# Post-LN transformer layer on one NeuronCore: attention sums of the first layer kept beside each value, and divided after a transfer

## The reference

```python
    x = _layernorm(x + _L0_attn_ref(x, L0_attn_Wqkv, L0_attn_Wo, L0_attn_bo), axis=-1)
    x = _layernorm(x + _L0_ffn_ref(x, ...), axis=-1)

    # _L0_attn_ref
        qkv = x @ Wqkv
        q = apply_rope(q)
        k = apply_rope(k)
        q = q / jnp.sqrt(jnp.sum(q * q, axis=-1, keepdims=True) + 1e-06)
        k = k / jnp.sqrt(jnp.sum(k * k, axis=-1, keepdims=True) + 1e-06)
        attn = jnp.einsum('bthd,bshd->bhts', q, k) / math.sqrt(HD)
        attn = jax.nn.softmax(attn, axis=-1)
        out = jnp.einsum('bhts,bshd->bthd', attn, v).reshape(b, t, d)
        return out @ Wo + bo
```

## Time and profile before

| | |
|---|---|
| median of 3 runs | 1354.19 us (1352.57 to 1356.01) |
| profiled execution, own time | 1358.76 us |
| its span, first to last instruction | 1357.0 us |
| TensorE busy | 1261.1 us, 93% |
| ScalarE busy | 922.6 us, 68% |
| VectorE busy | 793.4 us, 58% |
| GpSimd busy | 238.9 us, 18% |
| mean granted TensorE clock | 0.975 |

### The profile page before, as it was taken

The page is one execution under the profiler, slowest core; times in us unless marked ns, Lnnn a source line. Parts: engine busy times, 40 slices in busy tenths (PEclk is TensorE's granted clock), DMA queues, the critical chain, the costliest instruction groups (busy, mean ns, idle before and its releaser), DMA issues. The chain is left out here.

```text
span 1357.0 us, 20871 instructions
## 1 busy us (share of the span) xinstructions
PE 1261.1 (93%) x7142; PEld 673.0 (50%) x7142; DVE 793.4 (58%) x1876; ACT 922.6 (68%) x1634; POOL 238.9 (18%) x182
## 2 busy tenths in 40 slices
PE   5599999999999898999999999999987899999996
PEld 2133343343343333344434343444333799999996
DVE  5234455455451677787878787877863554444442
ACT  1388788787787465676667666766654477777775
POOL 3212212212211010011111111111101122122121
PEclk8799999999999899999999999999988999999998
DMA  4255342341333121223222222212368321112110
GB/s 156 75 140 109 103 140 65 107 140 59 113 127 95 52 87 63 74 69 87 71 86 72 78 80 68 90 51 92 123 205 231 111 66 57 53 52 59 55 51 5
DMA packets 101087, 122.60 MB, mean 90 GB/s; under 512 B 7347, under 2 KB 86835, under 8 KB 100980
## 3 DMA queue, kind: packets, MB, share of 16 engines
q1 hardware_dynamic: 79302, 89.12, 21.4%
q10 hardware_dynamic: 17248, 19.27, 4.8%
q0 software_dynamic: 4432, 12.87, 3.2%
HBM read 46.89 MB, written 24.27 MB: 52 GB/s over the span
## 5 line engine op out<-in xcount | busy, mean ns | idle before, releaser
L740 ACT ACTIVATE w_space<-bank 128x512 f32<-128x512 f32 x1024 | 560.4, 607 | 281.4 <-PE bank L497 273.3
L956 DVE TENSOR_REDUCE negm<-bank 128x1 f32<-128x512 f32 x512 | 334.1, 684 | 105.4 <-PE bank L529 102.9
L497 PE MATMUL bank<-w_space 96*128 96x512 bf16 (+1 forms) x1024 | 356.6, 387 | 31.2 <-DMA w_space<-work_space 16.0
L514 PE MATMUL bank<-w_space 128*32 128x512 f32 x2048 | 275.4, 610 | 0.2 <-ACT w_space L749 0.2
L497 PEld LDWEIGHTS bank<-w_space 96*128 96x128 bf16 (+1 forms) x1024 | 93.9, 99 | 309.7 <-ACT w_space L740 213.6
L529 PE MATMUL bank<-w_space 96*128 96x512 bf16 x512 | 198.3, 387 | 16.7 <-DVE negm L956 7.0
L692 PE MATMUL bank<-w_space,work_space 128*128 x624 | 141.0, 379 | 0.0
L560 PE MATMUL bank<-work_space,wqkv_sb 128*128 128x512 f32 x256 | 126.5, 620 | 9.4 <-DMA wqkv_sb<-in_w_qkv_dram 6.1
L692 PEld LDWEIGHTS bank<-w_space,work_space 128*128 128x128 f32 x624 | 115.6, 190 | 14.1
L1390 POOL TENSOR_TENSOR work_space<-w_space,work_space 128x1024 bf16<-128x1024 f32 x32 | 68.2, 2132 | 303.5 <-ACT work_space L791 185.2
L529 PEld LDWEIGHTS bank<-w_space 96*128 96x128 bf16 x512 | 50.4, 98 | 91.3 <-DVE negm L956 52.5
(11 more groups left out here) (162 smaller groups left out, 1350.7 us busy)
## 6 DMA issues: line engine op xcount, KB each, us to landing
w_space<-work_space SPq DMA_DIRECT2D x372, 128.0 KB
w_space<-in_w_dram SPq DMA_DIRECT2D x14, 1024.0 KB, 16.0
work_space<-rows_dram SPq DMA_DIRECT2D x39, 256.5 KB, 2.6
work_space<-in_x_t_dram ACTq DMA_DIRECT2D x8, 512.0 KB, 3.8
work_space<-in_x_dram ACTq DMA_DIRECT2D x8, 512.0 KB, 3.8
x_dram<-xo SPq DMA_DIRECT2D x16, 256.0 KB, 4.1
h_dram<-row_sb SPq DMA_DIRECT2D x16, 256.0 KB, 2.2
work_space<-h_dram ACTq DMA_DIRECT2D x8, 512.0 KB, 3.9
```

The lines of the kernel that those rows point to most:

```text
L497: nc.tensor.matmul(bank[:, :], k_stack[0:rows, b % 2, HEADS_AT_ONCE * g + j, kt * P:(kt + 1) * P], q_stack[0:rows, b % 2, HEADS_AT_ONCE * ...
L514: last = nc.tensor.matmul(pv_bank[VW * j:VW * (j + 1), :], v_aug[:, 1 - b % 2, at:at + VW], probs[:, q % PROBS, j, :], start=(kt == 0), st ...
L740: nc.scalar.activation(probs[:, q % PROBS, j, :], st_bank(b, c)[0][:, :], ACT.Exp, scale=SCALE).then_inc(exps, 1)
L956: ve.tensor_reduce(negm[:, c % TT, c // TT:c // TT + 1], mx_ring.bank(b, (g, c))[:, :], axis=AX.X, op=ALU.max, negate=True).then_inc(mx_ri ...
```

## The change

In the first layer the ones now stand beside each value: v_aug holds value, one, value, one, 32 columns per head, so that the attention matmul writes each output row and directly below it a row with the head's sum. ScalarE copies the bank as before, now into o_space. New tasks MV0 to MV3 on SyncE send, per group, the odd partitions (sums) to o_sums, a free part of row_sb, and the even ones (values) to o_rows, a view of on, where four groups make up 2 x 128 rows of channels by 512 tokens. New tasks ON0, ON1 on VectorE, each for two groups, take the reciprocal of 128x512 sums and multiply. That is already the transposed form which WO needs, so TO, TP and their evictions go in the first layer. MV0 of a batch waits for WO1 of the batch before, since the rows share memory. The second layer keeps its transposes and reads values and sums at a step of two.

The tables move WO0 from (9, 3) to (5, 2) and WO1 from (10, 2) to (6, 1). The nine padding transfers move from stage 2 to stage 1, since row_sb is used for sums from there on.

```diff
 ATTENDED = (
-    dict(TO0=(7, 3), TO1=(11, 3), TO2=(15, 3)),
+    dict(MV0=(6, 2), MV1=(9, 2), MV2=(13, 2), ON0=(15, 0)),
 FINISHED = (
-    dict(TO3=(2, 3), TP0=(4, 0), TP1=(6, 3), WO0=(9, 3), WO1=(10, 2), R1=(11, 1), N10=(12, 0),
+    dict(MV3=(1, 2), RS=(2, 3), ON1=(4, 0), WO0=(5, 2), WO1=(6, 1), R1=(11, 1), N10=(12, 0),
          N11=(12, 2), R2=(13, 1), N20=(14, 0), N21=(14, 2)),
...
+        o_sums = (row_sb[:, 1:3, D:2 * D], row_sb[:, 0:TT:3, D:2 * D])
...
+        o_rows = on[:, :, :].rearrange("p t d -> p (t d)").rearrange("p (u t) -> p u t", u=KD)
+        oT = o_space[:, :, :].rearrange("p s d -> p (s d)")
@@ TensorE: pv, WO @@
-                    at = (kt * H + HEADS_AT_ONCE * g + j) * VS
+                    at = (kt * H + HEADS_AT_ONCE * g + j) * VW
...
-                    pe.wait_ge(*ring.empty(b, f"TP{u}"))
+                    if second(b):
+                        pe.wait_ge(*ring.empty(b, f"TP{u}"))
+                    else:
+                        pe.wait_ge(on_ready, 2 * b + 2)
...
+                            rows = turned_of(u)[:, t, k, :] if second(b) else o_rows[:, k, at:at + P]
@@ ScalarE: group_out @@
-                if g:
+                if second(b) and g:
                     act.wait_ge(*o_ring.full(b, f"TO{g - 1}"))
-                elif b:
+                elif b > BATCH:
                     act.wait_ge(*o_ring.full(b - 1, f"TO{GROUPS - 1}"))
+                else:
+                    wait(act, o_moved, 32 * (GROUPS * b + g))
@@ VectorE @@
+                elif kind == "ON":
+
+                    dve.wait_ge(o_moved, 32 * (GROUPS * b + 2 * u + 2))
+                    stepping(ve.reciprocal(o_sums[u], o_sums[u]))
+                    all_steps()
+                    rows = o_rows[:, u, :].rearrange("p (a t) -> p a t", a=2)
+                    ve.tensor_tensor(rows, rows, o_sums[u], ALU.mult).then_inc(on_ready, 1)
@@ SyncE @@
+                elif kind == "MV":
+
+                    sp.wait_ge(oT_ready, GROUPS * b + u + 1)
+                    if b == 0 and u == 2:
+                        sp.wait_ge(padded, 16 * (E + 1))
+                    if b and u == 0:
+                        sp.wait_ge(*o_ring.full(b - 1, "WO1"))
+                    own = slice(u % 2 * (P // 2), (u % 2 + 1) * (P // 2))
+                    sp.dma_start(o_sums[u // 2][own], oT[1:P:2, :].rearrange("p (a t) -> p a t", a=2)
+                                 ).then_inc(o_moved, 16)
+                    sp.dma_start(o_rows[own, u // 2, :], oT[0:P:2, :]).then_inc(o_moved, 16)
...
-                if n == 2:
+                if n == 1:
                     sp.wait_ge(pad_set, 2)
```

49 lines of the change are left out of this document (25 added, 24 removed).

## The result

The changed kernel takes 1385.45 us (median), the kernel before 1354.5 in the runs beside it: a ratio of 1.021, 95% interval 1.019 to 1.024. It is slower by 31 us. One of the changed kernel's four executions took 4286.7 us, for a reason that its numbers do not show, and stays out of the ratio; the other three took 1381.3 to 1385.7. The prediction was 1356.8, range 1344 to 1367: wrong, with the time far above the range.

The account below looks back on a forecast made before the run. TensorE, busy 93% of the span, was taken as the bound. Start +8.5, stage 1 -1.3, stages 2 to 7 -6.6 and crossing +2 gave +2.6 on 1354.2: 1356.8 us, range 1344 to 1367.

Parts of the forecast that it names:

- Removed: On TensorE in each first-layer batch, six groups of four transposes go, 0.44 us each, 2.64 us in all.
- The waits are covered: Between nq and nk, the moved WO0 and WO1 let ScalarE catch up, removing TensorE's 1.31 us of waits per stage.
- The reciprocal: On VectorE, twice per batch, a reciprocal of 128x512 was put at 3.1 us from a row of 16 elements.
- both rivals on it: VectorE's reciprocal: 0.77 us giving about 1344 (chance 0.12), or 4.4 us giving 1365.4 (chance 0.20).
- on_ready and WO0: On TensorE, WO0 waits 1.6 us a stage for VectorE's on_ready at t = 20.1, all scores behind it.
- The stack copies: SyncE's copies start at t = 30.9 instead of 26.7; with MV1 between, the last k copy is issued at 47.3.
- The landing: The last k copy was taken to land 3 us after its issue, at t = 50.3, from other SyncE transfers' 2.2 to 4.1.
- The stage is 50.3 (49.0 to 51.4): Stages 2 to 7 end on the k stack at 50.3 us, 1.1 less each, -6.6 in all.
- The padding: At the start, padding stores moved to stage 1 hold batch 0's k copies: first score at 56, +8.5 (0 to +13).
- the rival of an undisturbed start: At the start, k copies hold their place beside the padding stores; first score near 47.4, total 1348; chance 0.18.
- Stage 1: Stage 1 has no WO and loses three TO groups of transposes: -1.3 us.
- The crossing: Stages 8 and 9, into the second layer: ON pairs +4.9, transpose groups -3.5, VectorE idle time hides a little: +2 (-3 to +5).

Follow-up runs that it names:

- experiment 1: Changed kernel with the nine padding stores made to wait for the first score of stage 1; 1381.2 us, 1.020 of the kernel before.
- experiment 5: Changed kernel with padding stores behind stage 1's first score, ON1 between kA's and kB's products, and WO1's addition behind lq except in the last first-layer batch; 1361.8 us.
- experiment 7: Changed kernel with only the last first-layer batch's division on ScalarE, as exp(-ln s), instead of VectorE's reciprocal; 1385.9 us, 1.025 of the kernel before.
- experiment 8: Kernel before with only the nine padding stores moved from stage 2 to the start of stage 1; 1364.2 us, 1.008 of the kernel before.
- experiment 3: Changed kernel with the first layer's reciprocals left out, rows multiplied by the sums; 1368.0 us, 1.008 of the kernel before.
- kernel 2: Changed kernel with WO0 and WO1 behind nq on TensorE and WO1's addition behind lq on VectorE; 1383.7 us, 1.023 of the kernel before.
- kernel 4: Changed kernel with the edits of experiment 1 and kernel 2 together; 1376.0 us, 1.017 of the kernel before.
- kernel 6: Experiment 5 with the whole first layer's division on ScalarE as exp(-ln s) instead of VectorE's reciprocal; 1360.2 us, 1.004 of the kernel before.
- kernel 9: Experiment 5 with ScalarE issuing the residual's load one quad later in the first layer; 1363.9 us, 1.008 of the kernel before.
- kernel 10: Kernel 9 with the last first-layer batch's division on ScalarE; 1355.9 us, 1.002 of the kernel before.
- kernel 11: Kernel 10 with the norm matmul nq and uq each one chunk sooner; 1357.1 us, 1.002 of the kernel before.
- kernel 12: Kernel 11 with MV1's two transfers issued by ScalarE behind its copy-out instead of by SyncE; 1365.5 us, 1.009 of the kernel before.

## Why the prediction was wrong

By its own steps:

- **Removed.** Transposes 2.64 us a stage: right. "The waits are covered", which took a further 1.31 off: this step failed. In the stage shown TensorE waits 0.8 us for exponentials and 0.2 for a copy-out by the list of waits, before it was 1.3; most of it now lies behind nk. The starts say more: TensorE arrives at t = 51.45 instead of 49.0, and of that 47.4 is the forecast's work and 1.6 the wait for on_ready, so 2.4 are left for ScalarE, where the sum had put nothing. Taking work from TensorE brings it to ScalarE's results sooner. The prediction took the distances from the earlier trace rows less what was removed, as if nothing else could come to bound; by this step alone the stages would have gained nothing.
- **The reciprocal.** Estimated at 3.1 from 16 elements, 3.34 measured, so 6.2 ns per element beyond some 160 ns (an estimate from the two rows). Right; both rivals on it fell. By the Trainium skill, VectorE: DVE Perf Modes, section First, the fixed hardware budget, the division is iterated; the reading of its repeat count of 8 as eight cycles an element would have given 4.4 us, and the row says 3.34.
- **on_ready and WO0.** Wait forecast 1.6, measured 1.41; on_ready at t = 20.1, measured 20.2, WO0 at t = 20.4. Right.
- **The stack copies.** Start at t = 30.9, measured 31.1. Then 12 copies "in 8.0", MV1 1.1, last k issue at 47.3: measured 8.5, 1.4, 48.3. One us short.
- **The landing.** "Its landing has no row; ... I take 3." The completions recorded in the trace of before say 3.9 to 4.8 in six of seven stages and 6.5 in one; in the stage shown it was 4.2. This was to be had ahead, and it is the term that was mis-sized: with 1.0 and 1.2 together the stack is at t = 52.5 instead of 50.3, and the stage is 52.6, 1.2 longer than before instead of 1.1 shorter.
- **"The stage is 50.3 (49.0 to 51.4)."** The mechanism, a stage that ends on the k stack, was right. The range was not: it took the landing as a number. It differs from stage to stage (4.0 to 5.5 in the changed kernel), and a stage that ends on it pays its upper side; in experiments 1, 5 and 7 a fall of the clock came behind some of the long waits on top, in the changed kernel's own stages 2 to 6 none did. Stages 2 to 6: -5.5 forecast, +7.5 measured. This and the crossing are the two terms that put the time outside the range.
- **The padding.** +8.5 forecast, +8.85 measured at the first score, and alone (experiment 8) +7.6 there and +9.4 on the medians. Right, and the rival of an undisturbed start fell, and with it what the prediction had drawn from the round robin in the Trainium skill's DMA: Bandwidth & Descriptors, section Queues, rings and completion order: the k copies stood on the other queue, and the first score came 9 us late. What was priced was the delay; what made it avoidable, one wait (experiment 1), I had not named.
- **Stage 1.** -1.3 forecast, -0.6 by the start of stage 2 and -1.5 by its next copy-out. Right.
- **The crossing.** +2 (-3 to +5) forecast, +9.6 measured. This step failed. The sum itself does not give +2: 4.9 less 3.5 is 1.4, and what VectorE's idle time hides makes it less. It also counted eight transpose groups and two ON pairs where nine and three fall into the stretch; the third pair, at 434 us, holds nothing that the waits show. The failure is of kind, though: the sum counted VectorE's added and TensorE's removed time as one queue. The maxima have two banks: a block of 4.0 or 5.4 us on VectorE stops TensorE for what two banks do not cover, 2.6 and 4.6 us, wherever VectorE is idle later; the removed transposes do not make up for it. The granted clock was lower too (0.90 over the crossing, 0.95 before), but only part of this goes with the reciprocals: without them it is 0.92 (experiments 3 and 7). In experiment 3 the crossing is 8.7 shorter without reciprocals, and over all kernels 6 with the last batch's gone (experiment 7).
- **No copy-out waits for a transfer**, **the second layer's stages unchanged**: both right.

Of 31 us on the medians, 8 to 10 are the padding (experiment 8 and the first scores) and 12 to 17 the reciprocals (experiment 3). The remaining 4 to 11 are what the transfers, the order of the additions and the waits for ScalarE cost over what the transposes gave back, and up to 3 us of chance in the expert part. This last is a difference, not a measurement, and its parts stay open. Open too is why some landings of the k copies take 6 to 9 us, the longest always in stage 3 of kernels 2, 4, 5, 6 and 9 to 12; the load's time is not the cause.

## What to carry to other kernels

Before removing work from the engine that bounds, list how much slack each of its inputs has at that moment, in us: here 3.5 for the stack and 0 for the exponentials, so a change that lengthens the chain to the first by 4.7 loses 1.2, and the 2.6 that it takes off the engine itself go into waits for the second. Price a long instruction by the banks that stand between it and the engine that it feeds, not by its engine's idle share: sixteen times 3.34 us on a VectorE that is 40% idle cost 12 to 17 us.
